# Layer 0 of a four-layer graph network: three of eight row blocks masked by an accumulating matmul on TensorE instead of by VectorE's clip against a tensor of bounds

## The reference

```python
q = (x @ Wq.T + bq).reshape(B, N, H, Dh).transpose(0, 2, 1, 3)      # k and v alike
scores = einsum('bhnd,bhjcd->bhnjc', q, kc) / sqrt(Dh)
scores = clip(scores, -10.0, 10.0)
scores = where(mask == 0, -10.0, scores)
attn = softmax(scores, axis=-1)
ctx = einsum('bhnjc,bhjcd->bhnd', attn, vc)
out = ctx @ Wo.T + bo + x                                            # then a layer norm with gamma, beta
```

## Time and profile before

| what | us |
|---|---|
| median of 3 runs (range) | 2209.93 (2208.72 to 2213.47) |
| the profiled execution | 2215.57 |
| its span | 2213.8 |
| busy in the span: TensorE matmul, VectorE, ScalarE, GpSimd | 1753.8, 1727.9, 1300.1, 374.9 |
| all 256 clips of layer 0 (L638) | 397.5 busy, 1590 ns each |
| all 512 score matmuls of layer 0 (L386) | 163.9 busy |
| all 112 additions on GpSimd (L327) | 234.5 busy |

### The profile page before, as it was taken

How to read it: one execution, slowest core, us unless ns; L and a number is a source line. 1 busy time by engine, 2 the same in 40 slices (tenths; PEclk the granted TensorE clock), 3 DMA queues, 4 the chain that set the end, 5 groups by cost and what they waited for, 6 DMA issues and landing times. The chain is left out here.

```text
span 2213.8 us, 34593 instructions
## 1 busy us (share of the span) xinstructions
PE 1753.8 (79%) x12514; PEld 1036.7 (47%) x12514; DVE 1727.9 (78%) x2851; ACT 1300.1 (59%) x1679; POOL 374.9 (17%) x233
## 2 busy tenths in 40 slices
PE   2788788787888864779888977877778765999997
PEld 1233223232323223667677756655567653545554
DVE  1888898888888854578878889889798975677674
ACT  1655445454444414766767878888798853455553
POOL 0243433344443431000100000000000000000000
PEclk7899999998999975889999988988789986999999
DMA  8213031120302003111111112212122202000000
GB/s 230 65 39 77 1 77 39 40 65 13 77 21 57 1 0 108 39 39 49 46 41 41 49 39 69 77 60 67 52 68 69 77 31 81 10 10 10 19 10 19
DMA packets 50168, 109.51 MB, mean 49 GB/s; under 512 B 7152, under 2 KB 26224, under 8 KB 50000
## 3 DMA queue, kind: packets, MB, share of 16 engines
q1 hardware_dynamic: 50000, 107.25, 16.7%
HBM read 69.08 MB, written 4.59 MB: 33 GB/s over the span
## 5 line engine op out<-in xcount | busy, mean ns | idle before, releaser
L972 ACT ACTIVATE g<-s_all,steep_d 128x1024 fp8e4<-128x1024 f32 x608 | 642.3, 1135 | 43.8 <-DMA s_all<-s_rows 27.1
L913 PE MATMUL acc<-parts,g 128*128 128x102 bf16 (+1 forms) x6144 | 419.2, 229 | 29.3 <-DVE sums L1063 20.3
L913 PEld LDWEIGHTS acc<-parts,g 128*128 128x128 fp8e4 x6144 | 403.1, 100 | 62.6 <-issue 44.9
L638 DVE SCALAR_TENSOR_TENSOR e<-e,bound 128x1024 f32<-128x1024 f32 x256 | 397.5, 1590 | 7.0 <-ACT e L522 7.0
L895 PE MATMUL post<-parts,edge 128*128 128x396 bf16 (+1 forms) x1024 | 233.0, 384 | 86.8 <-DVE base L1071 86.8
L327 POOL TENSOR_TENSOR ctx_sb<-ctx_sb,chunk 128x512 f32<-128x512 f32 x112 | 234.5, 2094 | 392.3 <-DVE chunk L650 392.2
L528 ACT ACTIVATE chunk<-ctx_ps 128x512 f32<-128x512 f32 x128 | 76.4, 597 | 361.9 <-POOL ctx_sb L327 296.3
L1056 DVE TENSOR_TENSOR g<-g,edge 128x1024 int32<-128x1024 int32 x192 | 228.0, 1220 | 36.5 <-ACT g L972 36.5
L522 ACT ACTIVATE e<-s_ps 128x1024 f32<-128x1024 f32 x256 | 247.7, 1023 | 5.8 <-PE s_ps L386 3.3
L403 PE MATMUL ctx_ps<-inv_sum,spread 128*128 128x512 f32 x256 | 154.8, 689 | 65.3 <-ACT chunk L528 40.4
L409 PE MATMUL ctx_ps<-e,v 128*32 128x512 f32 x1024 | 144.0, 633 | 65.4 <-DVE chunk L650 61.8
(11 more groups left out here) (134 smaller groups left out, 2233.9 us busy)
## 6 DMA issues: line engine op xcount, KB each, us to landing
s_all<-s_rows SPq DMA_DIRECT2D x96, 512.0 KB, 3.7
qs<-split SPq DMA_DIRECT2D x128, 128.0 KB, 2.4
ks<-split SPq DMA_DIRECT2D x128, 128.0 KB, 2.3
x<-in_x SPq DMA_DIRECT2D x8, 512.0 KB, 8.0
adj_in<-in_adj SPq DMA_DIRECT2D x8, 512.0 KB, 4.0
out_x<-x SPq DMA_DIRECT2D x8, 512.0 KB, 3.2
parts<-in_adj_t SPq DMA_DIRECT2D x6, 512.0 KB, 6.5
chunk<-in_adj_t SPq DMA_DIRECT2D x4, 512.0 KB, 7.2
```

The lines of the kernel that those rows point to most:

```text
L638: dve.scalar_tensor_tensor(out=tile, in0=tile, scalar=CLIP_LO, in1=lim, op0=ALU.max, op1=ALU.min).then_inc(p_ready, 1)
L913: ins = pe.matmul(self.acc[:, bank, o:o + self.NS], self.g[:, h % RING, jt, it * P:(it + 1) * P], self.upper[par][:, jt, h, :, :].rearrang ...
L972: act.activation(self.g[:, h % RING, jt, :], self.s_all[:, h % 2, :], ACT.Relu, bias=self.steep_d[par][:, jt, h:h + 1], scale=STEEP, satur ...
```

## The change

For the row blocks 1, 4 and 7 (six of the sixteen steps: 1, 4, 7, 9, 12, 15) the mask moves into the scores. Each of the four score matmuls of such a block is followed by a second one that accumulates into the same PSUM region: the stationary operand `minus` is -1e30 times the identity (bfloat16), the moving operand `lost` is 128.0 where there is no edge and 0 elsewhere (8-bit float). The exponential of such a score is 0, and the clip becomes a `tensor_scalar` with two immediate numbers and no second tensor. The bounds shrink to five blocks, in one raising instruction over all of them, and the first pass is done per row block.

```diff
+    MASKED = (1, 4, 7)
+    CLIPPED = tuple(t for t in range(T) if t not in MASKED)
...
-        bound = sb("bound", [P, T, N])
+        bound = sb("bound", [P, len(CLIPPED), N])
+        lost = sb("lost", [P, len(MASKED), N], F8)
+        minus = sb("minus", [P, P], BF16)
...
                     ins = pe.matmul(s_ps[:, hp, j, :], ks[par][:, 2 * hp + j, jt * P:(jt + 1) * P],
-                                    qs[par][:, 2 * hp + j, half * HALF:(half + 1) * HALF], start=True, stop=True)
+                                    qs[par][:, 2 * hp + j, half * HALF:(half + 1) * HALF], start=True,
+                                    stop=jt not in MASKED)
+                    if jt in MASKED:
+                        ins = pe.matmul(s_ps[:, hp, j, :], minus[:, :],
+                                        lost[:, MASKED.index(jt), half * HALF:(half + 1) * HALF], start=False, stop=True)
...
-                act.wait_ge(bounded, 2)
+                act.wait_ge(bounded, 3)
...
-                some = bound[:, 4 * part:4 * part + 4, :]
-                dve.tensor_scalar(some, adj_in[part], 0, CLIP_HI, ALU.not_equal, ALU.mult).then_inc(bounded_above, 1)
-                dve.wait_ge(bounded_above, part + 1)
-                dve.tensor_scalar(some, some, CLIP_LO, None, ALU.max).then_inc(bounded, 1)
+                for t in range(4 * part, 4 * part + 4):
+                    if t in MASKED:
+                        ins = dve.tensor_scalar(lost[:, MASKED.index(t), :], adj_in[part][:, t % 4, :], 0, EDGE,
+                                                ALU.is_equal, ALU.mult, saturate=False)
+                    else:
+                        ins = dve.tensor_scalar(bound[:, CLIPPED.index(t), :], adj_in[part][:, t % 4, :], 0, CLIP_HI,
+                                                ALU.not_equal, ALU.mult)
+                ins.then_inc(bounded, 1)
+
+            def raise_bounds():
+                dve.wait_ge(bounded, 2)
+                dve.tensor_scalar(bound[:, :, :], bound[:, :, :], CLIP_LO, None, ALU.max).then_inc(bounded, 1)
...
+                dve.tensor_scalar(minus[:, :], c.ident[:, :], NEG, None, ALU.mult)
...
                 bounds(0)
                 bounds(1)
+                raise_bounds()
                 finish_additive_weights()
-                dve.wait_ge(bounded, 2)
+                dve.wait_ge(bounded, 3)
...
                 tile = e[:, 2 * (i % 2) + hp, :, :]
-                lim = bound[:, jt, half * HALF:(half + 1) * HALF].unsqueeze(1).to_broadcast([P, 2, HALF])
+                if jt in MASKED:
+                    dve.tensor_scalar(tile, tile, CLIP_LO, CLIP_HI, ALU.max, ALU.min).then_inc(p_ready, 1)
+                    return
+                lim = bound[:, CLIPPED.index(jt), half * HALF:(half + 1) * HALF].unsqueeze(1).to_broadcast([P, 2, HALF])
                 dve.scalar_tensor_tensor(out=tile, in0=tile, scalar=CLIP_LO, in1=lim, op0=ALU.max,
                                          op1=ALU.min).then_inc(p_ready, 1)
```

More of the change, by code:

```diff
@@ L223, in layer0 @@
         x_loaded = [c.sem(f"x_loaded_{k}") for k in ("0", "1", "2_on")]
-        adj_loaded, bounded_above = [c.sem("adj_loaded_a"), c.sem("adj_loaded_b")], c.sem("bounded_above")
+        adj_loaded = [c.sem("adj_loaded_a"), c.sem("adj_loaded_b")]
         bounded, consts, ident0 = c.sem("bounded"), c.sem("consts"), c.sem("ident_zeroed")
```

## The result

The changed kernel takes 2188.44 us (median of 4 runs, 2183.49 to 2189.03), and the kernel before, on the same chips, 2211.7 us: a ratio of 0.9888 (95% interval 0.9864 to 0.9912), 23 us less. The prediction said 2204.9 us and a range of 2193 to 2220: the right way, but too little, and the time lies outside the range.

What follows compares the result with a forecast made beforehand. TensorE and VectorE were both taken as near full in layer 0, the bound changing by step. Savings of -22.3 and costs of +16.5, then +1.5 and -0.7, gave -5.0 from 2209.93: 2204.9 us, range 2193 to 2220.

Steps and rivals of the forecast that it cites:

- the price of the mask matmul: Score matmuls on TensorE: 0.235 us per added mask matmul (bounds 0 and 0.30), 0.94 us for four.
- rival 2: TensorE becomes the bound, at 0.34 us per mask matmul: about +10, 2220 us; chance 0.20, slower.
- The pair of clips: VectorE, two shortened clips with a GpSimd addition beside them: 2.45 us instead of 3.45, 1.0 us less.
- steps 4, 6, 7, 14 and 15: Layer 0, mostly over seven stages: -7.0, +5.9, -6.3, +6.0 and -7.0 us, in that order.
- Layers 1 to 3: The layers behind layer 0: not touched by the change, 0.
- another layer's time moves: Sign in the profile after, outside layer 0: if it occurs, the prediction is wrong.
- Rival 1: Idle behind both updates shrinks enough that TensorE keeps its higher clock afterwards: about -12, 2198 us; chance 0.20, faster.
- step 5: Layer 0, TensorE behind `update`: half of the 0.58 us over a plain step goes away, -2.0 us over seven stages.
- step 1: Layer 0: the clips get shorter, but TensorE sets the pace, so 0.
- Step 3: Layer 0: mask matmuls against TensorE's slack of 0.61 us; +0.3 each or 0 where `act_h` holds it, +1.4 us in all.
- Step 8: Layer 0: masks cost 0.94 us less TensorE's 0.40 wait for inverse sums, 0.54 x 6, +3.2 us.
- The first stage and the setup: First graph's masked blocks and shorter clips +1.5 us; the setup's shorter instructions -0.7 us.

Runs made afterwards that it cites:

- the padding: Kernel before with 128 semaphore increments at the head of TensorE's program, no work changed: 2205.81 us, ratio 0.9964; with 288 increments 2221.57 us, ratio 1.0046.
- the two profiles of the kernel before: The unchanged kernel profiled at first and once more for a second profile; the repeat measured 2209.90 us, ratio 0.9994.
- blocks 4 and 7: The full change for row blocks 4 and 7 only, without block 1: 2192.51 us, ratio 0.9916.
- the padded changed kernel: The full change with 128 semaphore increments at the head of TensorE's program: 2191.51 us, ratio 0.9893.
- masks only: Kernel before plus the mask matmuls of all three blocks (with block 7's pattern), old clips kept: 2218.33 us, ratio 1.0025.

## Why the prediction was too small

What was right: the price of the mask matmul (0.235 predicted, 0.23 measured), so rival 2, which needed 0.28 or more, fell, as did the 131 ns that the Trainium skill gives (TensorE: Matmul & The Clock Gate, "Back-to-back issue gap"). The pair of clips (2.45 predicted, 2.37 measured), with GpSimd shut out in turn as before; a pair of the new clips takes 1.28 without an addition and 2.37 with one. By that, the trace agrees with the Trainium skill on the shared pair of ports (SBUF — State Buffer, "Who interferes with whom") for the `tensor_scalar` too. And five terms of the sum within 0.8 us: steps 4, 6, 7, 14 and 15.

What was wrong, in the order of size:

- **Layers 1 to 3 "are not touched: 0".** This term failed most: they gave 10.6 us in the two profiles, and that another layer's time moves stood in the prediction as a sign that it is wrong. Some 6.9 of them are the one stall for code that the longer program of TensorE removes; the padding shows this without any change of work. The other 3.7 are no more than this part differs from run to run: 2.6 between the two profiles of the kernel before, and 1373.7 (blocks 4 and 7) against 1383.6 (the padded changed kernel) where the stall is gone. TensorE's clock is at its lower level for 306 and 296 us of this part in the two profiles of the kernel before, for 292 with the full change and for 305 with the padded full change, so this too moves without a change of work.
- **Rival 1 was no rival but part of the result.** I gave the clock half of step 5 and nothing at step 1. Step 1 brought 2.7 (block 1's masks in step 0 keep the clock up: masks only is 2.0 under blocks 4 and 7 there) and step 5 all of its 3.8. Against the second profile of the kernel before it is 2.3 and 3.1, so up to 1.1 of the two is how that first profile fell. I had written that TensorE idles through `update` at step 15 and so the clock would fall; it does fall there still, but it is back a step earlier.
- **Step 3, +1.4 predicted, -1.0 measured.** I costed step 1's shorter clips at nothing, since TensorE sets that step's pace. But the statistics on VectorE come behind them, and GpSimd's roots behind those. In the full change they are done before the clips of step 2 begin (its `weigh` is the row at 429.37, and the clips come behind it):

```profile
425.16 1.28 DVE L656 TENSOR_SCALAR e<-e 128x1024 f32<-128x1024 f32 x2
...
427.36 1.65 POOL L116 TENSOR_TENSOR rstd<-var_eps,mhalf 128x8 f32<-128x8 f32 x1 [7.47 <-DVE var_eps L111]
...
429.08 0.20 POOL L118 TENSOR_TENSOR offset<-minus_mean,rstd 128x8 f32<-128x8 f32 x1
429.37 0.69 DVE L671 TENSOR_TENSOR chunk<-chunk,ctx_ps 128x512 f32<-128x512 f32 x1 [2.09 <-PE ctx_ps L411]
```

  The masks-only kernel has the old clips in step 1. There the second operation of the roots (L118) comes later than the `weigh` of step 2, behind the first clip of that step, and takes 1.11 instead of 0.20:

```profile
442.42 1.65 POOL L116 TENSOR_TENSOR rstd<-var_eps,mhalf 128x8 f32<-128x8 f32 x1 [8.53 <-DVE var_eps L111]
...
443.37 0.69 DVE L668 TENSOR_TENSOR chunk<-chunk,ctx_ps 128x512 f32<-128x512 f32 x1 [1.03 <-PE ctx_ps L411]
...
444.15 1.11 POOL L118 TENSOR_TENSOR offset<-minus_mean,rstd 128x8 f32<-128x8 f32 x1
```

  ScalarE's `act_h` waits for these roots, and where they are this late, step 3 takes 5.37 and more instead of 4.84. It is so in six of seven graphs with masks only (+2.6), and in two of the three graphs of the kernel before whose step 1 had the higher clock: a short step 1 leaves the roots no time. With the shorter clips the roots are in time however short step 1 is, and step 3 is at -1.0. So this term and that of the clock at step 1 can't be added up one by one: the clips turn the clock's gain into time. The saving was real, only two steps and two engines further on.
- **Step 8, +3.2 predicted, +1.5 measured.** I subtracted the 0.40 that TensorE waits for the inverse sums, but missed a second slack, its wait for `weigh` within the same step (0.21 us before `values` in the fifth graph).

The first stage and the setup (+0.8 predicted) came to +0.3 at the ninth step; the second profile of the kernel before has 1.2 more there than the first, so this term can't be told from nothing. So in the steps of layer 0 the sum was short by 9 us through the clock (about 4.5, or 3.4 against the second profile), step 3 (2.4), step 8 (1.7) and some smaller terms, and outside layer 0 by the 10.6.

## What to carry to other kernels

Work that is added in the idle time of TensorE can give back a part of its cost, because the clock level behind it stays up (the masks cost 9.4 us in the steps where the prediction had 16.5, with 5.7 given back at steps 1 and 5): look at the granted clock in the steps behind every idle before costing an addition. When an instruction gets shorter in a step that another engine bounds, follow what is queued behind it on its own engine through the next two steps before writing 0. And before believing a gain of a few us, compare the parts of the kernel that the change doesn't touch: if one of them moved by a lump, pad the program and see.

## What the runs showed of the hardware

The load of program code can stall TensorE by 5 us in the middle of a loop: 55 us against 48.3 for one graph of layer 1, with five loads of 16 KB against none in the DMA view, in all three profiles with the old TensorE program and in none of the nine whose program is longer. Whether it is the place of the loop's end in the loaded pieces that decides is not shown. A semaphore increment costs TensorE's queue 0.15 us, so 288 of them cost 43 us of its time, of which 18 showed. And a bfloat16 matmul with an 8-bit moving operand and a weight load of its own, between two float32r matmuls, costs 0.23 us for 512 columns: the change of types costs nothing that can be seen.
